# Adapter, quantised FFN and residual: three sequences in one software pipeline, weight pieces transposed into PSUM

## What is computed

```python
def fake_quant(x):                       # per row
    s = jnp.maximum(jnp.max(jnp.abs(x), -1, keepdims=True) / 127.0, 1e-8)
    return jnp.clip(jnp.round(x / s), -127.0, 127.0) * s

y = jnp.einsum('bij,bkj->bik', x, weight[ids])       # x (8, 256, 1024), weight (16, 1024, 1024)
h = layernorm(y) * gamma + beta
h = jax.nn.gelu(fake_quant(h) @ fake_quant(w1).T + b1, approximate=False)
h = fake_quant(h) @ fake_quant(w3).T + b3            # w1, w3 (1024, 1024)
out = x + h
```

## Time and profile before

| | us |
|---|---|
| median of 3 runs | 415.48 |
| lowest, highest | 414.76, 419.6 |
| span of the profiled execution, first to last instruction | 413.9 |
| busy in it: TensorE, VectorE, GpSimd, ScalarE | 349.4, 355.9, 291.2, 228.8 |
| mean granted TensorE clock, share of full speed | 0.937 |

### The profile page before, as it was taken

How to read it: one execution, slowest core, us unless ns; L and a number is a source line. 1 busy time by engine, 2 the same in 40 slices (tenths; PEclk the granted TensorE clock), 3 DMA queues, 4 the chain that set the end, 5 groups by cost and what they waited for, 6 DMA issues and landing times.

```text
span 413.9 us, 5331 instructions
## 1 busy us (share of the span) xinstructions
PE 349.4 (84%) x1735; PEld 236.8 (57%) x1752; DVE 355.9 (86%) x320; ACT 228.8 (55%) x220; POOL 291.2 (70%) x143
## 2 busy tenths in 40 slices
PE   4999486889969898898799987999699969999755
PEld 4788364557545655666375745666475737575322
DVE  1987699889859998999899989999899979966796
ACT  3399463647547285546817474549635782735331
POOL 1414038244599859976599689996899689995970
PEclk9999868989998989899999996999899998999969
DMA  7999981459556984388906994589617991170112
GB/s 251 383 392 238 217 248 29 109 118 247 110 101 136 300 175 101 77 187 265 175 5 140 302 172 95 101 213 265 130 35 153 313 185 26 51 254 1 51 52 101
DMA packets 78616, 67.32 MB, mean 163 GB/s; under 512 B 3078, under 2 KB 71686, under 8 KB 78602
## 3 DMA queue, kind: packets, MB, share of 16 engines
q1 hardware_dynamic: 78602, 67.14, 64.7%
HBM read 58.74 MB, written 8.39 MB: 162 GB/s over the span
## 4 chain that ended last, share of the span: by engine, by line
POOL 34%; issue 9%; DVE 5%; ACT 2%; PE 1%; POOLq 0%
POOL o L427 7%; POOL y L418 7%; POOL x_res L437 6%; POOL a L443 6%; POOL y L420 4%; POOL o L431 2%; DVE a L902 2%; ACT y L545 2%; PE y_ps L1012 1%; POOL rstd L408 1%; POOL y L499 1%; DVE a L898 1%; POOL y L497 1%; POOL var_eps L404 0%; DVE g_half_max L907 0%
## 5 line engine op out<-in xcount | busy, mean ns | idle before, releaser
L994 PE MATMUL y_ps<-w_hi,x_hi 128*128 128x512 f32 x256 | 111.3, 435 | 29.9 <-DVE x_lo L753 18.1
L996 PE MATMUL y_ps<-w_hi,x_lo 128*128 128x512 f32 x256 | 105.9, 414 | 0.0
L995 PE MATMUL y_ps<-w_lo,x_hi 128*128 128x512 f32 x256 | 105.9, 414 | 0.0
L731 DVE TENSOR_TENSOR w_lo<-w_t,w_hi 128x2048 fp32r<-128x2048 f32 x28 | 93.0, 3322 | 6.5 <-ACT w_hi L512 6.3
L1012 PE MATMUL y_ps<-w_q,q_t 128*128 128x512 bf16 x369 | 85.3, 384 | 6.7 <-ACT q_t L562 4.6
L994 PEld LDWEIGHTS y_ps<-w_hi,x_hi 128*128 128x128 f32 x256 | 52.1, 204 | 47.2 <-issue 28.3
L725 DVE STREAM_TRANSPOSE w_t<-w_nat 128x2048 f32<-128x2048 f32 x28 | 64.5, 2305 | 5.1 <-DMA w_nat<-in_L_cond_weight 4.4
L1012 PEld LDWEIGHTS y_ps<-w_q,q_t 128*128 128x128 bf16 x384 | 36.5, 99 | 49.1 <-issue 9.1
L512 ACT ACTIVATE w_hi<-w_t 128x2048 fp32r<-128x2048 f32 x28 | 53.6, 1913 | 16.0 <-DVE w_t L725 16.0
L996 PEld LDWEIGHTS y_ps<-w_hi,x_lo 128*128 128x128 f32 x256 | 51.5, 201 | 11.9
L995 PEld LDWEIGHTS y_ps<-w_lo,x_hi 128*128 128x128 f32 x256 | 52.0, 203 | 10.7 <-issue 0.5
(11 more groups left out here) (107 smaller groups left out, 460.7 us busy)
## 6 DMA issues: line engine op xcount, KB each, us to landing
w_nat<-in_L_cond_weight SPq DMA_DIRECT2D x112, 256.0 KB, 4.7
x_res<-in_x SPq DMA_DIRECT2D x7, 1024.0 KB, 8.5
out<-o SPq DMA_DIRECT2D x14, 512.0 KB, 6.2
w_nat<-in_x SPq DMA_DIRECT2D x24, 256.0 KB, 5.8
w_nat<-in_L_cond_weight SPq DMA_DIRECT2D x8, 512.0 KB, 8.2
w_q<-in_L_ffn_w SPq DMA_DIRECT2D x4, 512.0 KB, 9.9
o<-in_L_ffn_w SPq DMA_DIRECT2D x4, 512.0 KB, 9.9
o<-in_x SPq DMA_DIRECT2D x2, 512.0 KB, 4.5
```

Of the source, the lines that this page charges most:

```text
L731: dve.tensor_tensor(w_lo[:, u], w_t[:, u % 2], w_hi[:, u].bitcast(F32), ALU.subtract).then_inc(w_lo_ready, 1)
L994: pe.matmul(ps, hi, w_hi[:, u, c], start=begin, stop=False)
L995: pe.matmul(ps, hi, w_lo[:, u, c], start=False, stop=False)
L996: last = pe.matmul(ps, lo, w_hi[:, u, c], start=False, stop=end)
```

## The change

Sequences now overlap three deep. In `period(p)` TensorE makes the adapter product of p, the first FFN product of p - 1 and the second of p - 2. Each unit of w is handled as two pieces of 1024 columns. VectorE transposes a piece from `w_nat` straight into PSUM (`t_ps`, 4 banks, 2 for each piece), and both the copy to `w_hi` (ScalarE) and the subtraction to `w_lo` (VectorE) read it there; `w_t` is gone. The other 4 banks are `a_ps` (one half of y for both tiles) and `f_ps`, which the transposes of h and g and all FFN products share. x has buffers of its own in SBUF (`x_nat`, `x_t`), so it is loaded a period earlier, and `low_x` is made by GpSimd. The rounded h has its own buffer `h_r`. The straight code at the start is longer (sequences 0 to 2, with the preparation of w1 and w3 spread through them; sequence 0's four units each have a buffer, and its loads stand ahead of all weight tiles of w1 and w3); the loop covers periods 3 to 6. `last_period` makes the adapter product of 7 by tiles (first all units for tile 0, then for tile 1), and interleaves what is left of the FFN of 5, 6 and 7. The scale rows are made by eight transposes instead of a product with ones.

```diff
+        a_ps = psum("a_ps", [P, TT, BANK])
+        f_ps = psum("f_ps", [P, KH, BANK])
+        t_ps = psum("t_ps", [P, NK, CP, BANK])
...
+            def store(b, t):
+                sp.wait_ge(out_ready, TT * b + t + 1)
+                dst = out[bass.ds(b, 1), t * P:(t + 1) * P, :].rearrange("o p d -> (o p) d")
+                sp.dma_start(dst, o[:, t, :]).then_inc(stored[t], 16)
+
+            def period(p):
+                load_unit(p + 1, 0)
+                load_unit(p + 1, 1)
+                store(p - 2, 0)
+                load_unit(p + 1, 2)
+                store(p - 2, 1)
+                load_residual(p - 1)
+                if not (isinstance(p, int) and p + 2 > LAST):
+                    load_x(p + 2)
+                load_unit(p + 1, 3)
 
...
-            load_first_units((0, 1))
+            load_first_unit(0)
+            load_first_unit(1)
             for k, src in enumerate((gamma, beta, b1, b3)):
                 sp.dma_start(rows_1[k], src.rearrange("(o n) -> o n", o=1)).then_inc(rows_loaded, 16)
+            load_first_unit(2)
+            load_first_unit(3)
             load_prep(range(0, 4))
-            load_first_units((2,))
+            load_x(1)
+            load_unit(1, 0)
             load_prep(range(4, 8))
-            load_first_units((3,))
-            load_prep(range(8, 12))
-            load_units(1, (0,))
-            load_x(1)
-            load_units(1, (1,))
-            load_prep(range(12, 16))
-            load_units(1, (3, 2))
-            iteration(1)
...
+            def low_x(b, ch):
+                half = slice(CU * ch, CU * (ch + 1))
+                pool.wait_ge(x_hi_ready, CH * (b - 1) + ch + 1)
+                pool.tensor_tensor(x_lo[:, half], x_t[:, half], x_hi[:, half].bitcast(F32), ALU.subtract
+                                   ).then_inc(x_lo_ready, 1)
+
...
+            def period(p):
+                add_b1(p - 2, 1)
                 for t in range(TT):
-                    pool.wait_ge(ffn1_scaled, KH * (TT * f + t + 1))
...
-            def iteration(b):
-                scale_and_shift(b - 1)
-                if is_second(b):
-                    diagonal(1)
-                if not isinstance(b, int) or 2 <= b:
-                    finish(b - 2)
-                add_b1(b - 1)
-                residual(b - 1)
-                normalisers(b)
+                    scale_and_shift(p - 1, t)
+                for t in range(TT):
+                    finish(p - 2, t)
+                low_x(p + 1, 0)
+                add_b1(p - 1, 0)
+                residual(p - 1)
+                normalisers_of(p)
+                low_x(p + 1, 1)
...
+            def period(p, units):
+                u0, u1, u2, u3 = units
+                normalise(p - 1, 0)
+                normalise(p - 1, 1)
+                split_w(*u0, 0)
+                take_g(p - 2, 0)
+                gelu(p - 2, 1)
+                split_w(*u0, 1)
+                round_g(p - 2, 1)
+                scale_ffn2(p - 2, 0)
+                round_h(p - 1, 0)
+                split_w(*u1, 0)
+                take_g(p - 2, 1)
+                split_w(*u1, 1)
+                round_h(p - 1, 1)
+                copy_y(p, 0)
+                scale_ffn2(p - 2, 1)
+                split_w(*u2, 0)
+                split_w(*u2, 1)
+                take_h(p - 1, 0)
+                split_x(p + 1, 0)
+                split_w(*u3, 0)
+                split_w(*u3, 1)
+                take_h(p - 1, 1)
+                gelu(p - 1, 0)
+                copy_y(p, 1)
+                round_g(p - 1, 0)
+                split_x(p + 1, 1)
...
+            def transpose_w(b, u, k):
+                n = piece_no(b, u, k)
                 dve.wait_ge(w_loaded[u % 2], 16 * NQ * (2 * (b - 1) + u // 2 + 1))
-                wait_past(dve, w_lo_ready, n - 2)
-                if u == 2 and not is_second(b):
-                    dve.wait_ge(x_lo_ready, HALVES * b)
-                dve.transpose(w_t[:, u % 2].rearrange("p c (kb s) -> p kb c s", s=BLK),
-                              w_nat[:, u % 2].rearrange("p kb (c r) -> p kb c r", r=BLK)
+                if isinstance(b, int) and n < NK:
+                    dve.wait_ge(first_lo_ready, len(FIRST))
+                else:
+                    dve.wait_ge(w_lo_ready, n - 1)
+                dve.transpose(t_ps[:, k].rearrange("p c (kb s) -> p kb c s", s=BLK),
+                              w_nat[:, u % 2].rearrange("p kb (c r) -> p kb c r", r=BLK)[:, :, blocks_of(k)]
                               ).then_inc(w_transposed, 1)
...
+            def low_w(b, u, k):
+                dve.wait_ge(w_hi_ready, piece_no(b, u, k) + 1)
+                dve.tensor_tensor(w_lo[:, u, blocks_of(k)], t_ps[:, k], w_hi[:, u, blocks_of(k)].bitcast(F32),
+                                  ALU.subtract).then_inc(w_lo_ready, 1)
...
+            def period(p, units):
+                u0, u1, u2, u3 = units
+                rescale1(p - 2, 1)
+                both(transpose_w, *u0)
+                low_w(*u0, 0)
+                scales_g(p - 2, 1, a[:, 1, :], 1)
+                low_w(*u0, 1)
+                scales_h(p - 1, 0, 0)
+                both(transpose_w, *u1)
+                scales_h(p - 1, 1, 1)
+                both(low_w, *u1)
+                statistics(p, 0)
+                both(transpose_w, *u2)
+                both(low_w, *u2)
+                transpose_x(p + 1)
+                both(transpose_w, *u3)
+                rescale1(p - 1, 0)
+                both(low_w, *u3)
+                scales_g(p - 1, 0, a[:, 0, :], 0)
+                statistics(p, 1)
+                mean_and_variance(p)
+
...
+            def period(p):
+                piece(p, 0, 0)
+                transpose_g(p - 2, 0)
+                piece(p, 0, 1)
+                ffn2(p - 2, 0)
+                piece(p, 1, 0)
+                transpose_g(p - 2, 1)
+                piece(p, 1, 1)
+                ffn2(p - 2, 1)
+                piece(p, 2, 0)
+                transpose_h(p - 1, 0)
+                piece(p, 2, 1)
+                ffn1(p - 1, 0)
+                piece(p, 3, 0)
+                transpose_h(p - 1, 1)
+                piece(p, 3, 1)
+                ffn1(p - 1, 1)
+
```

1411 lines of the change are left out of this document (730 added, 681 removed).

## The result

The changed kernel takes 410.25 us (median of 20 runs, 405.16 to 416.03) against 414.78 us of the kernel before (20 runs). The ratio is 0.985, 95% interval 0.982 to 0.988: 1.5% faster, clear of noise but small, where 381 us and 8% had been forecast. The forecast was wrong, and its range of 364 to 402 us does not hold the time.

The account below looks back on a forecast made before the run. Before, three engines were nearly full, VectorE most, with VectorE and GpSimd locking each other out; afterwards GpSimd's ring would set the period. 136 + 4 x 41 + 79 = 379 us of span, so 381 us; range 364 to 402.

Parts of the forecast that it names:

- rival (b): Hand-overs of pieces between VectorE and ScalarE cost: periods of 43.5 to 45 us, time 399 to 410 us; chance 0.17.
- Part 4: Start up to the first loop period: VectorE's 112 us of work plus waits, 136 us, ends 128 and 140.
- 8 us for one load: Head: VectorE waits about 8 us from 13 us on for the first two weight tiles, loaded behind sequence 0's w.
- 8 for the rest: Head: 8 us for other idle VectorE time, where the kernel before had 20 us.
- Part 1: Loop: transpositions into PSUM take 1.2 us, subtractions 1.22; VectorE's list per period 33.6 us instead of about 41.
- Rival (c): VectorE's transposition into PSUM runs at half pace, 2.3 us: period 47 us, time 433 us; chance 0.07.
- Part 2: Loop: x_lo moves to GpSimd, 35 us of work there, whose chain over the residual load sets a 41 us period.
- The ring: GpSimd's cycle over the residual load: 30.2 us of work plus 10.3 to 11.2 from finish to use, 40.5 to 41.4.
- rival (a): Residual load comes in time and TensorE sets the period: 38.5 us, time 362 us; chance 0.14.
- My price of 9 us for x_lo on VectorE: Loop: with x_lo left on VectorE, the sum would be 4 x 2.3 = 9 us shorter, 372 us.
- Part 3: Loop, three sequences deep: no TensorE wait over 1 us but the ring's, so the clock should hold.
- Part 5: End behind the loop: 62.5 us of TensorE work, 11 of waits, 4 behind the last matmul; 79 us, ends 75 and 84.

Follow-up runs that it names:

- e1: Changed kernel with SyncE's load of w unit (3, 1) issued ahead of the store of output tile (0, 0): 399.99 us, ratio 0.962.
- e11: e1 with only a sixteenth of sequence 1's weight units and an eighth of sequence 2's x transferred: 385.31 us.
- e14: e9 with loads of w unit (1, 3) ahead of weight tiles 9 to 12 and unit (2, 2) ahead of sequence 0's residual: 387.39 us, ratio 0.936.
- e13: e9 with w3's last weight tiles prepared in another order ahead of the loop, and unit (2, 2) loaded before sequence 0's residual: 390.48 us, ratio 0.944.
- e15: e13 with only part of the transfers of sequence 1's weights and sequence 2's x: 378.19 us.
- e8: Changed kernel whose loop subtraction for w_lo reads a constant in SBUF instead of the piece in PSUM: 439.63 us.
- e4: Changed kernel without the third product (w_hi by x_lo) of each step in the four loop periods: 410.25 us.
- e7: e1 with the residual loaded in two halves, each issued once its tile is finished, and the first half added ahead of x_lo: 395.2 us, ratio 0.945.
- e3: Changed kernel with the loop's two x_lo subtractions done by VectorE again instead of GpSimd: 410.61 us, ratio 0.984.
- e5: e1 with GpSimd's residual of sequence 6 moved behind the three additions of b1 at the end: 402.44 us, ratio 0.962.
- e12: e7 with ScalarE's copy of the last transposed h tile ahead of gelu of sequence 6's second tile: 394.32 us.
- e6: e5 with sequence 6's last two tiles rescaled by VectorE from PSUM instead of by ScalarE and GpSimd: 397.55 us, ratio 0.958.
- e10: e4 with the residual loaded in halves, the move of e7 alone, without e1: 406.36 us.
- e9: Changed kernel with the moves of e1, e5, e6 and e7, plus ScalarE's last transposed h copy ahead of gelu: 392.1 us, ratio 0.944.

## Why the prediction was wrong

The sum was 136 + 164 + 79 = 379 us of span. The trace of the changed kernel has 161.8 + 155.6 + 85.9 = 403.3. So the head was forecast 26 us too short, the loop 8 too long, the end 7 too short. That trace is of the fastest of 20 executions; the median is 5 us longer, which makes the miss larger, not smaller. That 410.25 us falls on the upper end of rival (b) is chance: its longer periods did not come.

**Part 4, the start, is the step that failed.** Its list of VectorE's work was good: 112 us by it, 108.7 us busy by the trace. The terms behind it were not: 8 us for one load and "8 for the rest", where VectorE stands idle for 161.8 - 108.7 - 8.3 = 44.8 us. The one load was not where I had it: VectorE reads the first two weight tiles at 20.3 us without a wait for them, and stands 3.7 us ahead of that for `x_hi`. "8 for the rest" came from the idle time of the kernel before, though the change had moved the loads and one more sequence's work into the head. Two causes are shown. First the place of `store(0, 0)` ahead of the load of unit (3, 1): 9 to 10 us (e1; 71.4 against 61.8 to 62.3 between the marks). I listed VectorE's work in the head without walking SP's list beside it, as I had done for the loop. Second the transfers: 9.5 us in the changed kernel's own trace (the mark of sequence 1 at 92.3, in e11 at 82.8), 13 to 17 in the other pairs, of which the order of loads gives back some 3 (e14). I had a rate in my own rows (204 GB/s over the head) and counted 2 MB for one wait; 17.5 MB stand up to unit (1, 3), and VectorE transposes it at 68.7 us: 255 GB/s. The two causes are 19 of the 26 us: e11, without either, starts the loop at 142.6 us. What is left against 136, some 6 to 7 us, is open. It is not the order of w3's preparation (e13, e15).

**Part 1, w pieces through PSUM, was right.** Transposition 1236 ns (1.2 taken), subtraction 1216 (1.22), VectorE 32.2 us of a period (33.6). e8 puts the price on it: 26 us over the loop, with the rest of the change in place. Rival (c) is excluded by the first row, rival (b) by the periods.

**Part 2, x_lo on GpSimd.** The ring was right in kind and its load mis-sized: 7.3 to 9.8 us from `finish` to use, not 10.3 to 11.2. The period is 38.8 on average (36.8 to 40.1), not 41. So rival (a)'s 38.5 came true in the loop, with a correction: TensorE does not set the period alone. Without 7.3 us of its work the period stays (e4), and with the ring shorter it falls to 38.2 (e7). My price of 9 us for x_lo on VectorE fell to 2.2 us in the loop and none in the time (e3). The Trainium skill, "GPSIMD Engine Reference", section "4.1 Engine selection", would leave it on VectorE, GpSimd being about twice slower with two inputs. The trace agrees on the pace (x_lo takes VectorE 1.2 to 1.4 us in e3 and GpSimd 2.4); the time tells the two placements apart in neither direction (0.984 against 0.985), since both hide under TensorE.

**Part 3, three deep.** TensorE waits 2.7 us for copies of transposed g in four periods, 1.2 at the longest, where it stood 4.1 us for x_lo in one period before, and the clock is 1.00 through the loop: nearly as forecast (I had allowed no wait over 1 us but the ring's).

**Part 5, the end.** 85.9 us against 79 and an upper end of 84. The waits that I walked are there (2.65, and 3.42 for the last h tile against 4.2), and more that I had put at "some 4": 1.8, 2.8 and 2.2 us. I left out what follows a wait: TensorE's granted clock is 0.50, its lower level (1.2 GHz), from 368 to 376 us, and 16 matmuls there take 5.33 us instead of 3.63. I also left out the lock, which Part 1 takes out of the loop and which here makes five VectorE operations two to three and a half times as long (2.42 us against 0.69 for one of the last additions). Of the repairs, e5 turned a wait into lock and e12 moved one by a product; only e6, which took work off GpSimd, shortened the end, by 3 us in its trace.

## What to carry to other kernels

Walk every queue through the straight code ahead of the loop as through the loop itself, the DMA issuer's above all, and look for a store that stands ahead of a load that another engine needs. Deepening a pipeline moves work and transfers out of a loop into its head and end; sum the bytes that must arrive by each point and divide by the rate that the trace shows, before counting any engine's work there. Where two limits lie within a microsecond of each other, taking work off one may show nothing (e3, e4), while shortening the one that varies can give more than its mean (e7). A lighter kernel can also bring up waits that the full one does not have (e10).

## What the runs showed of the hardware

- The transposition on VectorE writes to PSUM at the pace at which it writes to SBUF: 1236 ns for 1024 elements a partition, 2305 ns for 2048 before.
- The same subtraction of 1024 elements beside a busy GpSimd: 1212 ns with one input in PSUM, 2196 ns on average with both in SBUF, in one kernel (e8). With both in SBUF and GpSimd out of its way it takes 1.2 to 1.4 us (e3).
- The waits behind the loads of the first 80 us differ from run to run by up to 7 us at equal order (the mark of sequence 1 at 92.3 to 99.5 us), while the four loop periods together (151.2 to 151.3 us) agree to 0.1 us in e7, e9, e12, e13, e14 and e15.
